# A kernel whose fixed order is played a second time to place products of constants

## The reference

```python
qkv = h @ W_qkv (+ b);  s = einsum('bqhd,bkhd->bhqk', q, k) / 4
x = x + gate * (softmax(s) @ v) @ W_o         # full, or windows of 128 in layer 2
x = x + gate * cross(q, context, top-k 16 in layer 2) @ W_co
x = x + gate * (act(h @ W1 + b1) @ W2 + b2)   # silu(a) * b in layer 2
```

## Time and profile before

| | |
|---|---|
| three runs | 3048.83, 3053.17, 3050.72 us, median 3050.72 us |
| the profiled execution | 3054.61 us, span 3052.8 us |
| mean granted clock of TensorE | 0.95 |
| TensorE matmuls | 92% of the span, 14941 recorded |
| VectorE, ScalarE, GpSimd | 66%, 46%, 21% |
| products of constants (L1235) | 1620 |
| chain that ended last | TensorE 71%, VectorE 13%, issue 7%, DMA 4% |

### The profile page before, as it was taken

One profiled execution on the slowest core, in us unless ns is written; L12 is line 12 of the kernel. 1 busy time (PEld: TensorE's weight loads), 2 busy tenths in 40 slices (PEclk: granted clock), 3 DMA queues, 4 the chain that ended last, 5 costly groups with the idle time before them and its releaser, 6 DMA issues.

```text
span 3052.8 us, 47858 instructions
## 1 busy us (share of the span) xinstructions
PE 2798.3 (92%) x14941; PEld 1347.5 (44%) x14996; DVE 2007.6 (66%) x4848; ACT 1401.3 (46%) x2571; POOL 638.1 (21%) x967
## 2 busy tenths in 40 slices
PE   8899999999999998999988888889889998999899
PEld 5433334335536323334465566565542432332456
DVE  6778477643683865884365678676878584886631
ACT  3255635663443762664634233322215355577341
POOL 1010001121410110132134345324321000112320
PEclk9799989999999998999998999999998999899899
DMA  6323122323451322243176326421331041122521
GB/s 186 109 66 113 42 63 66 117 78 90 149 157 46 91 60 62 67 126 97 44 194 183 117 71 172 130 87 37 108 88 49 15 126 50 41 59 84 183 99 37
DMA packets 268156, 286.80 MB, mean 94 GB/s; under 512 B 70665, under 2 KB 207243, under 8 KB 267275
## 3 DMA queue, kind: packets, MB, share of 16 engines
q1 hardware_dynamic: 256651, 282.28, 31.4%
q0 software_dynamic: 11264, 1.46, 0.3%
HBM read 167.43 MB, written 114.72 MB: 92 GB/s over the span
## 4 chain that ended last, share of the span: by engine, by line
PE 71%; DVE 13%; issue 7%; DMA 4%; ACT 2%; POOL 2%; SPq 1%; DVEq 0%; ACTq 0%; POOLq 0%
PE ring_c L1404 11%; PE ring_b L1371 11%; PE ring_a L1327 11%; PE ring_a L1439 7%; PE ring_b L1427 7%; PE ring_a L1416 4%; PE ring_b L1370 3%; PE ring_b L1284 3%; DVE row_max L1689 2%; ACT probs L1512 2%; PE ring_b L1398 2%; PE ring_a L1427 1%; PE ring_a L1299 1%; DMA q_ring<-neg_max_parts 1%; PE ring_b L1249 1%
## 5 line engine op out<-in xcount | busy, mean ns | idle before, releaser
L1512 ACT ACTIVATE probs<-ring_b 128x512 f32<-128x512 f32 (+1 forms) x1728 | 906.4, 602 | 518.0 <-PE ring_b L1371 453.9
L1689 DVE TENSOR_REDUCE row_max<-ring_a 128x1 f32<-128x1024 f32 x512 | 603.6, 1219 | 153.5 <-PE ring_a L1327 148.8
L1371 PE MATMUL ring_b<-q_ring,k_ring 100*128 100x512 bf16 x1536 | 521.8, 388 | 30.0 <-ACT probs L1512 13.4
L1327 PE MATMUL ring_a<-k_ring,q_ring 96*128 96x512 bf16 x1536 | 491.5, 414 | 37.9 <-DVE row_max L1689 17.9
L1404 PE MATMUL ring_c<-probs,v_and_ones 128*17 128x512 f32 x3072 | 402.3, 601 | 4.7 <-ACT probs L1512 4.6
L1795 POOL CAST neg_max_parts<-neg_max 16x128 bf16<-16x128 f32 x112 | 33.0, 295 | 1633.3 <-ACT neg_max L1506 1299.4
L1686 DVE CUSTOM_DVE_ANT_0 w_mlp<-ring_a,w_mlp 128x1024 bf16<-128x1024 f32 x256 | 302.7, 1222 | 60.5 <-PE ring_a L1327 58.7
L1327 PEld LDWEIGHTS ring_a<-k_ring,q_ring 96*128 96x128 bf16 x1536 | 131.0, 100 | 375.7 <-issue 295.5
L1371 PEld LDWEIGHTS ring_b<-q_ring,k_ring 100*128 100x128 bf16 x1536 | 144.4, 99 | 328.9 <-issue 228.1
L1733 DVE TENSOR_TENSOR x_tok<-x_tok,ring_a 128x512 f32<-128x512 f32 x96 | 66.0, 687 | 336.8 <-PE ring_a L1439 207.1
L1427 PE MATMUL ring_b<-h_feat,w_mlp 128*128 128x512 f32 x512 | 229.2, 594 | 3.9 <-ACT h_feat L1483 1.7
(11 more groups left out here) (145 smaller groups left out, 3496.6 us busy)
## 6 DMA issues: line engine op xcount, KB each, us to landing
q_ring<-scr_q SPq DMA_DIRECT2D x128, 384.0 KB, 4.3
scr_q<-split SPq DMA_DIRECT2D x64, 384.0 KB, 2.6
k_ring<-scr_k SPq DMA_DIRECT2D x64, 384.0 KB, 5.1
scr_q<-split SPq DMA_DIRECT2D x64, 256.0 KB, 3.0
scr_out<-out_stage SPq DMA_DIRECT2D x128, 128.0 KB, 2.6
scr_out<-out_stage SPq DMA_DIRECT2D x64, 256.0 KB, 2.2
h_feat<-scr_out SPq DMA_DIRECT2D x56, 256.0 KB
reciprocals<-scr_recip SPq DMA_DIRECT2D x56, 256.0 KB
```

What stands on the lines that cost most here:

```text
L1327: last = mm(ps[:, half * BLOCK:(half + 1) * BLOCK], q[0:PARTS, h, t * P:(t + 1) * P], k_view(g)[0:PARTS, h, half * BLOCK:(half + 1) * BLOC ...
L1371: last = mm(ps[:, :], k_view(g)[0:ROWS, h, s.kt * P:(s.kt + 1) * P], q[0:ROWS, h, q0:q0 + BLOCK], start=not g.masked, stop=True)
L1512: f(PT[0:n, s.pt, :], ps[0:n, :], ACT.Exp, **kw).then_inc(b_evac, 1)
L1689: v.tensor_reduce(NM[:, s.nm, s.u:s.u + 1], ps, AX.X, ALU.max).then_inc(a_evac, 1)
```

## The change

`fill` no longer takes the planner's times. It plays the fixed order again: each engine takes its steps in order, each step starts when the steps that it waits for have ended, when its engine is free and when its ring place is free. Planned engine durations are multiplied by 1.03 (`SLOW`), the planned latencies of transfers by 1.3 (`FAR`). The gap is then the time between the moment at which engine and ring place are both free, and the step's start. The threshold 0.8, the 0.3, the share 0.7 and the 0.11 stay. The order of the steps, all real instructions, all tiles and all waits stay.

```diff
+FAR, SLOW = 1.3, 1.03
 def fill(steps):
-    end = 0.0
+    free = dict.fromkeys(("PE", "ACT", "DVE", "POOL", "SP"), 0.0)
+    ring = dict(a=[0.0] * A_SLOTS, b=[0.0] * B_SLOTS)
+    end, table = dict(), None
     for s in steps:
-        eng, us = s["ph"][0]
-        if eng == "PE":
-            gap = s["t0"] - end
-            s["fill"] = int((gap - 0.3) * FILL_SHARE / FILL_ONE) if gap > FILL_LEAST and s.get("ring") else 0
-            end = s["t0"] + us
+        at = max([end[id(x)] for x in s["after"] if x is not None and id(x) in end] + [0.0])
+        r, prev = s.get("ring"), None
+        if r:
+            at = max(at, ring[r][0])
+        if s["t0"] < 60.0 and s["ph"][0][0] == "SP":
+            at = max(at, s["t0"])
+        for n, (eng, us) in enumerate(s["ph"]):
+            at = max(at + (LINK[prev] if n else 0.0), free[eng])
+            if n == 0 and eng == "PE":
+                gap = at - max(free[eng], ring[r][0] if r else 0.0)
+                s["fill"] = int((gap - 0.3) * FILL_SHARE / FILL_ONE) if gap > FILL_LEAST and r else 0
+            if s["kind"] in ("root", "ctx_root"):
+                table = "exp"
+            elif eng == "ACT" and "fn" in s and s["fn"] != table:
+                table, us = s["fn"], us + 1.3
+            at += us * SLOW
+            free[eng], prev = at, eng
+        if r:
+            ring[r].pop(0)
+            ring[r].append(at + LINK[prev])
+        end[id(s)] = at + (s["lat"] * FAR if s.get("lat") is not None else LINK[prev])
```

## The result

The changed kernel takes 3067.81 us in the median of 5 runs (3066.76 to 3079.12) against 3050.72 us (3046.13 to 3057.34, 5 runs) for the kernel before. The ratio is 1.0064 with a 95% interval of 1.0041 to 1.0088: 0.6% slower, 17 us in the medians. The forecast was 3065 us, with a range of 3045 to 3084.

The account below looks back on a forecast made before the run. TensorE was taken to bound the kernel, with 71% of the chain. Removals -15.3, additions +30.0, +1.0 and +1.4 gave +17.1 us; with -3 for the clock, +14 us on the median of 3050.72: 3065 us, range 3045 to 3084.

Parts of the forecast that it names:

- The additions without a wait: At 41 steps with no TensorE wait, on the chain, 274 products lose 30.0 us; two half-covered steps lose 1.0 us.
- second rival: Additions on TensorE's chain are absorbed because a second chain is close behind: no change, 3050 us, chance 0.14.
- The removals: At 24 steps on the chain, 139 products taken away at 0.110 us each gain 15.3 us.
- the nine turns and the 25: Layer 2 MLP loop turns losing 35 products in all, and 25 products at 2247 removed from the chain.
- both engines have slack in the loop: Argument against the third rival (removals do not pay, 3080 us, chance 0.20): TensorE and VectorE wait in turn.
- The clock: Two to four restarts at half clock saved by filled waits, one or two new ones: net -3 us.
- The restart price: After the 5.23 us wait, slower transposes (0.93 us) and following records (1.02 us) make a restart cost 1.9 us.
- The additions off the chain: At 19 steps without a wait, chain elsewhere, 137 products: value 0 except at 714, bound 13.5 us lost.
- The sum at 714: 26 more products before the output product delay TensorE by 2.86 us, and the gate after it: 1.4 us lost.
- That the change does not do what it says: Second playing should leave only true waits but does not at 41 places; the forecast itself, chance 0.58.
- the first rival: The clock pays: eight restarts saved and 88 to 126 at full clock give 3040 us, faster; chance 0.08.
- The rival beside it: The rival that the clock pays: filled waits save all eight restarts, 15.6 us; 3040 us, chance 0.08.

Follow-up runs that it names:

- e3: Kernel before, with the larger of old and new numbers only at the 43 steps where TensorE had no wait, 1911 products: ratio 1.0063.
- e5: Kernel before, with all 287 removals made and products added only at the 34 steps inside true waits, 1502 products: ratio 0.9980.
- e9: Kernel before, with the additions at the 43 no-wait steps doubled, 582 instead of 291, 2202 products: ratio 1.0141.
- e1: Kernel before, each step with the smaller of old and new numbers, so only the 287 removals, 1333 products: ratio 0.9997.
- e11: Kernel before, all removals but at 13 steps where the clock fell, additions only inside true waits, 1604 products: ratio 0.9979.
- e4: Kernel before, with only the 169 additions at the 34 steps inside waits of the trace, 1789 products: ratio 0.9987.
- e13: Kernel before, each step with the larger of the old number and the number from measured waits, 2379 products: ratio 0.9937.
- e2: Kernel before, each step with the larger of old and new numbers, so only the 597 additions, 2217 products: ratio 1.0057.
- e6: Kernel before without any products of constants: ratio 1.0040.
- e10: Kernel before, with products only at 92 steps whose measured TensorE wait was over 0.4 us, 1778 products: ratio 0.9936.

## Why the prediction was right

The result lies within 3 us of the forecast, and that is luck in part: the place and the cause of the loss were right, but two terms were wrong by 12 and 14 us and cancel.

- **The additions without a wait** were the main term, and their place and sign were right: e3 and e5 put the loss there. The size was too large: 30.0 + 1.0 us forecast, 19 us (14 to 25) measured. Each product does cost 0.110 us where it stands, as the chain at 945 shows, and up to 1250 the whole of e3 and e9 shows that price. Behind 1250 it does not. The clock of e3 is 0.954, that is 0.003 over before, some 18 us less at half clock and by the estimate above 5 to 6 us, about half of the difference. The other half stays open; slack in other engines, which the forecast named in its second rival, was not isolated.
- **The removals** failed as a step: 15.3 us "gained", 0.9 us measured (between 5 gained and 3 lost). At the loops the turn is shorter by 0.29 us instead of 0.44. From 2215 to 2600, with the nine turns and the 25 (60 products, 6.6 us by the forecast), e1 and the changed kernel are 3.5 and 3.6 us shorter. At 2215 half clock takes what the removals would give. That half clock takes the rest everywhere fits e1's clock and is an estimate; e11, which was to test it, did not decide. The sentence that the nine turns and the 25 are on the chain was right, but it counted length alone. That both engines have slack in the loop, since they wait for each other in turn, was a wrong reading: the chain goes through both, so neither has any, and a turn became shorter as TensorE's part did.
- **The clock**, -3 us, agrees for the additions in waits (e4: 4 us faster, between 10 faster and 2 slower) and was wrong for the removals, where "one or two new" restarts were allowed: e1 spends some 55 us more at half clock.
- **The restart price** of 1.9 us holds: at the third place the e13 profile has the transposes 0.88 us shorter than before (1.09 for 1.97) and the output product 0.98 us (3.62 for 4.60). The assumption that 34 more products there would shorten the restart failed, as 2.94 us of wait stayed.
- **The additions off the chain** at value 0 (and 1.4 us at 714) cannot be read alone. The 428 additions outside waits cost 26 us between e5 and the changed kernel, the 291 of e3 cost 19 us, so the other 137 would cost some 6 us. By the other way, e2 less e3 and e4, it is 2 us. Both are smaller than their intervals. The bound was 13.5 us. The sum at 714 took 717.66 for an end without the modelled tail; that is the end with it. Without it is 717.50, and the sum gives 1.2 us for 1.4.
- **That the change does not do what it says**: shown. With FAR at 1.0 the new numbers are almost all removals, and the kernel is faster than before, not slower.
- **What would show it**: 1930 records, as forecast. TensorE busy 30 us longer, forecast 20 or more. A clock of 0.950 in the profile. The stretch from 88 to 126, which the first rival had at full clock, still has 0.50 (88 to 128 in the changed kernel). The stretch from 180 to 1250 longer than before: the same up products start at 946.76 in place of 926.41, 20.35 us later from the start of the span, of which 1.64 us are the fifteen products in front of them. At 180 us the changed kernel is 5.0 us behind, so some 15 us arise between there and 950. For 180 to 1250 the forecast had 12 less 3 us, and 14.5 were measured: the additions cost their length and the removals gave nothing there.
- The rule of the Trainium skill ("TensorE: Matmul & The Clock Gate", section "HAM oscillation — how this bites in real kernels"), that long idle gaps cost the clock, agrees with e6, e10 and e13 (0.912, 0.958 and 0.966). The rival beside it failed for this change: 16 of the 34 waits get only one or two products more, and at the one that gets most, 34, 2.94 us stay open with half clock behind. That waits of 0.55 us alone came before the fall at 402 is nearly so: 5 us earlier the timeline has one of 0.76 us.

## What to carry to other kernels

Work that only keeps the clock up is best placed by waits that a trace shows, and near to their end: here that gave 0.64%, while 2.94 us left open at one place lost the clock all the same. A planner's estimate with a safety factor on transfers places it where the engine is never idle, and there it costs up to its length, here 0.07 us of 0.11 on the average. When such work is removed, price the clock as well as the length: here the removals gave 0.9 us of 15.3.

## What was not expected

- Leaving 2.94 us of a long wait open gives half clock behind it, leaving 0.76 us gives the full clock, with 85 and 92 products ahead. That is one place in two executions; where between the two the limit lies, no run shows.
- All 1620 products together are worth 12 us net, though they stand for 60 us of the chain; the same kind of work placed by the trace is worth some 32 us against none at all (ratios 0.9936 and 1.0040, from different series).
- A product behind products of constants goes without the 0.09 us of issue and the 0.07 us of length that it shows after a wait, so removing 0.44 us of them gives 0.29 us.
